# Float32 transposes of rounded values, and unread bf16 products on TensorE, in a two-layer gated attention and FFN kernel

## The chip, the cores and the metric

The kernel runs on one NeuronCore of a Trainium2 chip. The metric is the device time of one launch in microseconds (us): the median of 3 runs of the kernel before is 760.56 us, the lowest 758.46, the highest 766.45.

## The reference, cut to what matters

x is [4, 512, 256] in float32, the context likewise. Two layers are computed, each of a gated cross-attention (16 heads of 16) and a gated feed-forward part. In layer 0 the latter is a mixture of 8 experts with the best two per token, in layer 1 a two-matrix FFN (256 to 1024 to 256) whose weights are rounded to -1, 0, 1 times a scale and whose activations are rounded to whole numbers per token. The rounded activations are what the change touches.

```python
def quant_act(x):
    scale = 127.0 / clip(max(abs(x), axis=-1), 1e-5, None)
    return clip(round(x * scale), -128.0, 127.0) / scale
def bitlinear(x, w): return einsum('bsi,oi->bso', quant_act(x), quant_weight(w))

x = x + tanh(g_xattn[0]) * attention0(layernorm(x), ctx, ctx)
x = x + tanh(g_ffn[0]) * experts(layernorm(x))
x = x + tanh(g_xattn[1]) * attention1(layernorm(x), ctx, ctx)
x = x + tanh(g_ffn[1]) * bitlinear(gelu(bitlinear(layernorm(x), w1)), w2)
```

## The kernel before, in words

There are 8 periods, one for each layer and batch element; periods 0 to 3 are the attention of layer 0, 4 to 7 that of layer 1. A period has 32 half steps, called slots here. `table()` writes the order of all work as one list, and every engine walks this same list and takes what is its own, so that each engine's queue is in the list's order.

In each slot TensorE (PE) does two score products of a later head ("S", line 778, into the three PSUM banks psS, 48 rows each), whose row maxima VectorE (DVE) reduces ("maxima", line 1215, one per product); two transposed score products ("T", line 792, into psT), whose exponentials ScalarE (ACT) writes to pt (line 1024); and in every second slot eight products with the values ("PV", line 806). S runs 12 slots ahead of T, so 12 slots of S alone stand ahead of slot 0 of period 0. There is one psT: the next T waits for the exponential of the one before. S waits for the reduction three products back. After the S of four heads, GpSimd (POOL) splits the maxima into two parts (mp, lines 669 and 672), PE transposes them (line 815, "MT"), ACT copies them to mt (line 1040), and a DMA adds them as rows to the queries, on which T waits.

All other work ("pieces") hangs on fixed slots by `work_table()`. Pieces use the two banks of psX in turn; PE's `bank()` waits until the piece before last has been read out. The pieces that the change and the prediction touch:

- SPLIT (line 731): a projection of keys or queries in float32, which ACT reads out twice (lines 971, 972); POOL subtracts to get the low part (line 595).
- LNC and LNN: the layer norm's numbers on POOL, its application on ACT (line 981, four tiles of 128 tokens, into xn).
- In periods 5 to 7 the FFN of the batch element just attended: XQ at slot 12 (DVE finds each token's scale, lines 1358 to 1368; POOL multiplies and adds a large constant, which rounds, line 678). XI at slot 14: ACT subtracts the constant and writes bf16 (line 1054). XB at slot 15: PE transposes eight 128x128 blocks (line 882), ACT copies them to xit (line 1064). F1 at slot 16: 16 bf16 products of 512 columns (line 903) and four Gelus on ACT (line 1075).
- For each of four token tiles t: HQ at slot 17+3t (DVE lines 1377 to 1387, POOL line 684 rounds hh in place), HS at 19+3t (ACT subtracts the constant and writes bf16 hq, line 1086), HT at 20+3t (eight PE transposes, line 913, and an ACT copy, line 1100), F2 at 21+3t (eight products, line 921; DVE adds, line 1397).

The last stage (NP = 8, after the last head) does the same for the last batch element with nothing beside it. There 45 unread bf16 products (BUSY, line 930) already run on PE.

## Time and profile before

| | us |
|---|---|
| median of 3 runs | 760.56 |
| lowest, highest | 758.46, 766.45 |
| the profiled execution's own time | 767.57 |
| its span (first to last instruction) | 764.9 |
| PE, DVE, ACT, POOL busy in the span | 691.0, 533.3, 445.5, 164.3 |

The profiled execution took 7.01 us more than the median, and 2.67 us of it lie around the span. All rows below are of this one execution. A busy PE is not a PE at its peak, since the records of pipelined products include their latency. The column PEclk is the clock granted to TensorE as a share of 2.4 GHz: 1.00 is 2.4 GHz, 0.50 is 1.2 GHz, and a value between is a mixture in time of the two.

### The profile page before, as it was taken

What the parts mean: (1) busy time and instruction counts of PE and PEld (TensorE: products, weight loads), DVE (VectorE), ACT (ScalarE), POOL (GpSimd) and SP (SyncE); (2) the same over time, 40 slices, a digit from 0 to 9 for tenths busy, and PEclk for the clock granted to TensorE, in tenths of its full rate; (3) what the DMA queues carried; (4) which work ended last, traced back from release to release, by engine and by line L of the source; (5) the groups of instructions that cost most, each with busy time, mean ns of one, the idle gap of its engine ahead of it and who ended that gap; (6) DMA issues with size and microseconds to landing.
All of it is one profiled execution on the core that took longest, in us unless ns stands there. A gap on an engine that the chain in (4) does not pass through costs nothing.

```text
span 764.9 us, 10167 instructions
## 1 busy us (share of the span) xinstructions
PE 691.0 (90%) x3595; PEld 327.5 (43%) x3600; DVE 533.3 (70%) x1140; ACT 445.5 (58%) x570; POOL 164.3 (21%) x300
## 2 busy tenths in 40 slices
PE   4899999899999999998999989998989898987786
PEld 2433333454544545444554545443444344432343
DVE  2767886568886778867887688765786668774334
ACT  2237766763346634664437634567776678658746
POOL 7115333620011210121101410213210311021132
PEclk9769999999999999999999999999999889978999
DMA  7948578430111610323210502126031402200000
GB/s 240 241 128 294 180 250 268 139 80 7 42 43 38 157 29 15 71 84 82 43 43 30 152 16 42 43 79 198 24 80 52 123 3 63 50 2 2 21 8 27
DMA packets 39026, 66.73 MB, mean 87 GB/s; under 512 B 5185, under 2 KB 13889, under 8 KB 38721
## 3 DMA queue, kind: packets, MB, share of 16 engines
q1 hardware_dynamic: 38128, 65.57, 30.2%
q8 instruction: 28, 0.46, 0.3%
q10 hardware_dynamic: 848, 0.53, 0.2%
q14 instruction: 22, 0.17, 0.1%
HBM read 38.29 MB, written 27.26 MB: 86 GB/s over the span
## 4 chain that ended last, share of the span: by engine, by line
PE 59%; DVE 14%; ACT 11%; issue 9%; POOL 8%; POOLq 0%; DVEq 0%; ACTq 0%
PE psO L806 11%; PE psS L778 8%; PE psX L731 7%; PE psT L792 6%; PE psX L867 5%; DVE mx L1215 5%; PE psX L843 4%; PE psX L868 4%; PE psX L869 4%; PE psX L751 3%; ACT pt L1024 3%; POOL parts L595 2%; DVE xs L1346 2%; ACT qf L971 2%; ACT parts L972 1%
## 5 line engine op out<-in xcount | busy, mean ns | idle before, releaser
L1024 ACT ACTIVATE pt<-psT 128x1024 f32<-128x1024 f32 x256 | 261.6, 1022 | 221.2 <-PE psT L792 218.6
L1215 DVE TENSOR_REDUCE mx<-psS 128x1 f32<-128x512 f32 x512 | 325.3, 681 | 84.0 <-PE psS L778 81.6
L778 PE MATMUL psS<-ks,qs 48*128 48x512 f32 x512 | 153.8, 518 | 15.5 <-DVE mx L1215 14.3
L806 PE MATMUL psO<-pt,vg 128*32 128x512 f32 x1024 | 142.0, 627 | 0.1
L792 PE MATMUL psT<-qs,ks 50*128 50x512 f32 x512 | 119.2, 433 | 9.6 <-ACT pt L1024 8.2
L778 PEld LDWEIGHTS psS<-ks,qs 48*128 48x128 f32 x512 | 60.7, 192 | 136.4 <-issue 75.7
L1346 DVE SCALAR_TENSOR_TENSOR xs<-psX,coef,xs 128x256 f32<-128x256 f32 x128 | 61.8, 483 | 32.4 <-PE psX L869 29.2
L595 POOL TENSOR_TENSOR parts<-qf,parts 128x512 fp32r<-128x512 f32 x30 | 38.4, 1280 | 152.5 <-ACT parts L972 152.5
L792 PEld LDWEIGHTS psT<-qs,ks 50*128 50x128 f32 x512 | 52.6, 191 | 28.1 <-ACT pt L1024 25.2
L867 PE MATMUL psX<-moeh,xh 128*128 128x512 f32 x128 | 57.4, 449 | 4.4 <-DVE xs L1346 4.4
L868 PE MATMUL psX<-moel,xh 128*128 128x512 f32 x128 | 51.0, 398 | 0.0
L869 PE MATMUL psX<-moeh,xl 128*128 128x512 f32 x128 | 50.4, 393 | 0.0
L669 POOL CAST mp<-mx 128x16 fp32r<-128x16 f32 x32 | 6.3, 197 | 173.5 <-DVE mx L1215 173.1
L731 PE MATMUL psX<-ctxb,wk 128*128 128x512 f32 x64 | 36.6, 705 | 7.3 <-DMA wk<-in_Wk 7.3
L867 PEld LDWEIGHTS psX<-moeh,xh 128*128 128x128 f32 x128 | 24.2, 189 | 43.6 <-DVE xs L1346 22.6
L981 ACT ACTIVATE xn<-xs,lnw 128x256 f32<-128x256 f32 x60 | 31.8, 591 | 15.2 <-POOL lnw L631 15.1
L806 PEld LDWEIGHTS psO<-pt,vg 128*32 128x32 f32 x1024 | 20.4, 109 | 44.6 <-issue 43.6
L684 POOL TENSOR_SCALAR hh<-hh,am 128x1024 f32<-128x1024 f32 x16 | 17.9, 1119 | 93.7 <-DVE am L1387 93.7
L731 PE MATMUL psX<-xnt,wq 128*128 128x512 f32 x64 | 32.8, 640 | 1.3 <-ACT xnt L994 0.8
L751 PE MATMUL psX<-wv,ctxb 128*128 128x256 f32 x128 | 33.0, 403 | 0.8 <-DVE parts L1171 0.8
L843 PE MATMUL psX<-wo,ont 128*128 128x256 f32 x128 | 31.6, 391 | 0.8 <-ACT ont L1017 0.8
L612 POOL TENSOR_SCALAR lnw<-mv 128x4 f32<-128x4 f32 (+1 forms) x17 | 3.9, 229 | 126.3 <-DVE mv L1138 125.7
(131 smaller groups left out, 764.1 us busy)
## 6 DMA issues: line engine op xcount, KB each, us to landing
ks<-kd SPq DMA_DIRECT2D x64, 192.0 KB, 3.6
qs<-qd SPq DMA_DIRECT2D x64, 192.0 KB, 4.5
kd<-parts SPq DMA_DIRECT2D x16, 512.0 KB, 3.2
qd<-parts SPq DMA_DIRECT2D x16, 512.0 KB, 2.7
kd<-parts SPq DMA_DIRECT2D x16, 256.0 KB, 3.7
qd<-parts SPq DMA_DIRECT2D x16, 256.0 KB, 3.4
ctxb<-in_ctxT SPq DMA_DIRECT2D x7, 512.0 KB, 4.5
xs<-in_x SPq DMA_DIRECT2D x4, 512.0 KB, 6.1
```

The lines of the kernel that those rows point to most:

```text
L731: i = mm(o, w[:, k, c * P:(c + 1) * P], src[:, k, :], start=k == 0, stop=k == NC - 1)
L751: i = mm(o[:, t * D:(t + 1) * D], ctxb[:, p % 2, k, (2 * half + t) * P:(2 * half + t + 1) * P], wv[l][:, k, :], start=k == 0, stop=k == NC ...
L778: mm(psS[:, i % 3, :], qs[at:at + KR, 2 * g + a, k * P:(k + 1) * P], ks[at:at + KR, 2 * g + a, :], start=True, stop=True).then_inc(pe_s, 1)
L792: i = mm(psT[:, r, :], ks[at:at + KR + MP, 2 * g + half, k * P:(k + 1) * P], qs[at:at + KR + MP, 2 * g + half, :], start=True, stop=True)
L806: i = mm(psO[32 * j:32 * j + 32, :], vg[:, p % 2, k, g * GH + j, :], pt[:, s % RING, j, :], start=k == 0, stop=k == NT - 1, tile_position= ...
L843: i = mm(o[:, t * D:(t + 1) * D], ont[:, k, tt * P:(tt + 1) * P], wo[l][:, k, :], start=k == 0, stop=k == NC - 1)
L867: mm(o, xh[:, k, tok], moeh[:, k, at], start=k == 0, stop=False)
L868: mm(o, xh[:, k, tok], moel[:, k, at], start=False, stop=False)
L869: i = mm(o, xl[:, k, tok], moeh[:, k, at], start=False, stop=k == NC - 1)
L1024: a(pt[:, G % RING, 2 * half:2 * half + 2, :], psT[:], ACT.Exp, scale=SCALE).then_inc(a_exp, 1)
L1215: v.tensor_reduce(mx[:, w // GH % 2, r, col:col + 1], psS[:, i % 3, :], AX.X, ALU.max).then_inc(v_max, 1)
L1346: v.scalar_tensor_tensor(out=xs[:, b, t, :], in0=o[:, k * D:(k + 1) * D], scalar=coef[:, t, e:e + 1], in1=xs[:, b, t, :], op0=ALU.mult, op ...
```

## The change

XI and HS go. PE transposes the rounded float32 values as they are (xn and hh, with the large constant in them), in twice the bytes, so that XB and HT become two pieces of four blocks each; ACT subtracts the constant while it reads PSUM and writes bf16. XB stands at slots 14 and 15 instead of 15, HT at 19+3t and 20+3t instead of 20+3t. The buffers hq and xi are gone, and xh has its own place in SBUF. Two new kinds exist on PE alone. WARM multiplies 512 columns of vg's bytes, as bf16, into psO: 20 ahead of the first S, then 3 after each of the 12 slots of S alone (36). FILL multiplies columns of w1q into the next bank of psX, after waiting until that bank has been read out, at 11 slots of each of periods 5, 6 and 7 (20 products a period, 60 in all). Nothing reads what they write.

```diff
@@ work_table(), periods of layer 1
             put(p, 12, ("XQ", (0, NT)))
-            put(p, 14, ("XI", (0, NT)))
-            put(p, 15, ("XB", (0, NT)))
+            put(p, 14, ("XB", (0, 1, 0, NT)))
+            put(p, 15, ("XB", (1, 2, 0, NT)))
...
                 put(p, 17 + 3 * t, ("HQ", (t,)))
-                put(p, 19 + 3 * t, ("HS", (t,)))
-                put(p, 20 + 3 * t, ("HT", (t,)))
+                put(p, 19 + 3 * t, ("HT", (t, 0)))
+                put(p, 20 + 3 * t, ("HT", (t, 1)))
...
+        if l:
+            for s, k in ((9, 2), (10, 2), (11, 3), (12, 2), (14, 2), (17, 1), (18, 3), (20, 2), (22, 1), (24, 1), (28, 1)):
+                put(p, s, ("FILL", (k,)))
+    for s in range(2 * LEAD):
+        put(lead, 2 * H - 2 * LEAD + s, ("WARM", (3,)))
...
-    put(NP, 6, ("HS", (0,)))
     for t in range(NT):
-        if t + 1 < NT:
-            put(NP, 6, ("HS", (t + 1,)))
-        put(NP, 6, ("HT", (t,)))
+        put(NP, 6, ("HT", (t, 0)), ("HT", (t, 1)))
@@ table(), ahead of the first slot
+    out += [("WARM", (20,))]
@@ PE
-            def xb(t0, t1):
-                o = bank("XB").bitcast(BF16)
+            def xb(c0, c1, t0, t1):
+                o = bank("XB")
                 w = (t1 - t0) * P
-                if due(a_xi, n("XB") + 1):
-                    pe.wait_ge(a_xi, n("XB") + 1)
-                for c in range(NC):
+                if due(p_xq, n("XQ tiles")):
+                    pe.wait_ge(p_xq, n("XQ tiles"))
+                for c in range(c0, c1):
...
-                        i = nc.tensor.transpose(o[:, at:at + P], xi[:, t, c * P:(c + 1) * P], identb[:])
+                        i = nc.tensor.transpose(o[:, at:at + P], xn[:, t, c * P:(c + 1) * P], identf[:])
...
+            def ht(t, half):
+                o = bank("HT")
+                if due(p_hq, n("HT") // 2 + 1):
+                    pe.wait_ge(p_hq, n("HT") // 2 + 1)
+                for k in range(NT):
+                    at = (half * NT + k) * P
+                    m = nc.tensor.transpose(o[:, k * P:(k + 1) * P], hh[:, t, at:at + P], identf[:])
...
+            def warm_up(k):
+                if due(c_pool, POOL_ALL):
+                    pe.wait_ge(c_pool, POOL_ALL)
+                for i in range(k):
+                    mm(psO[:], identb[:], vg[:, 1].rearrange("p t h d -> p (t h d)").bitcast(BF16)[:, 0:S],
+                       start=True, stop=True)
+
+            def fill(k):
+                b = n.piece() % 2
+                if due(*last[b]):
+                    pe.wait_ge(*last[b])
+                for i in range(k):
+                    mm(psX[:, b, :], identb[:], w1q[:, 0, 0:S], start=True, stop=True)
@@ ACT
-                a(xit[:, :, t0 * P:t1 * P], o.rearrange("p (c t) -> p c t", c=NC), ACT.Copy).then_inc(a_xb, 1)
+                a(xit[:, c0:c1, t0 * P:t1 * P], o.rearrange("p (c t) -> p c t", c=c1 - c0), ACT.Identity, bias=negm[:]
+                  ).then_inc(a_xb, 1)
...
-                a(hqt[:, i % 2].rearrange("p k t -> p (k t)"), o, ACT.Copy).then_inc(a_ht, 1)
+                a(hqt[:, i // 2 % 2, half * NT:(half + 1) * NT, :].rearrange("p k t -> p (k t)"), o, ACT.Identity,
+                  bias=negm[:]).then_inc(a_ht, 1)
```

How PE's queue changes at the head. Before, the transposes of the second layer norm were followed at once by the S of four heads (psS) and the transpose of their maxima (psX from mp):

```order
L762 MATMUL psX<-identf,xn 128x128 x8
L778 MATMUL psS<-ks,qs 128x512 x18
L815 MATMUL psX<-identf,mp 32x128
L778 MATMUL psS<-ks,qs 128x512 x8
L792 MATMUL psT<-qs,ks 128x512 x2
```

Now the same place reads (the pair of S and three products then repeats, up to the T of slot 0):

```order
L762 MATMUL psX<-identf,xn 128x128 x8
L926 MATMUL psO<-vg,identb 128x512 x20
L778 MATMUL psS<-ks,qs 128x512 x2
L926 MATMUL psO<-vg,identb 128x512 x3
L778 MATMUL psS<-ks,qs 128x512 x2
```

Twenty unread products stand between the transposes and the first S, and three behind every pair of S.

PE's queue in periods 5 and 6 from slot 14 to slot 16 before (the eight bf16 transposes at the end of slot 15):

```order
L778 MATMUL psS<-ks,qs 128x512 x2
L792 MATMUL psT<-qs,ks 128x512 x2
L778 MATMUL psS<-ks,qs 128x512 x2
L792 MATMUL psT<-qs,ks 128x512 x2
L806 MATMUL psO<-pt,vg 32x512 x4
L882 MATMUL psX<-identb,xi 128x128 x8
L778 MATMUL psS<-ks,qs 128x512 x2
```

and now:

```order
L778 MATMUL psS<-ks,qs 128x512 x2
L792 MATMUL psT<-qs,ks 128x512 x2
L880 MATMUL psX<-identf,xn 128x128 x4
L934 MATMUL psX<-w1q,identb 128x512 x2
L778 MATMUL psS<-ks,qs 128x512 x2
L792 MATMUL psT<-qs,ks 128x512 x2
L806 MATMUL psO<-pt,vg 32x512 x4
L880 MATMUL psX<-identf,xn 128x128 x4
L778 MATMUL psS<-ks,qs 128x512 x2
```

The first four transposes moved one slot earlier, ahead of S, T and PV of slot 15, and two unread products stand behind them.

ACT's queue for the first token tile, from the exponentials of slots 18 and 19 to that of slot 21, before:

```order
L1024 ACTIVATE pt<-psT 128x1024 x2
L1086 ACTIVATE hq<-hh,negm 128x1024
L1024 ACTIVATE pt<-psT 128x1024
L1040 ACTIVATE mt<-psX 32x128
L1100 ACTIVATE hqt<-psX 128x1024
L1024 ACTIVATE pt<-psT 128x1024 x2
```

and now (L1038 is the exponential, L1054 the copy to mt):

```order
L1038 ACTIVATE pt<-psT 128x1024 x2
L1099 ACTIVATE hqt<-psX,negm 128x512
L1038 ACTIVATE pt<-psT 128x1024
L1054 ACTIVATE mt<-psX 32x128
L1099 ACTIVATE hqt<-psX,negm 128x512
L1038 ACTIVATE pt<-psT 128x1024 x2
```

Two operations of 1024 columns became two of 512, at the same places.

## Rows read from the trace of the kernel before

**Rows 1.** The page: the chain that ended last, share of the span by engine.
```profile
PE 59%; DVE 14%; ACT 11%; issue 9%; POOL 8%; POOLq 0%; DVEq 0%; ACTq 0%
```

**Rows 2.** Stretches: length, busy PE, PEld, DVE, ACT, POOL (instructions), PEclk, DMA share, GB/s.
```profile
28.50:44.00 15.50, 14.32 (x29) 6.55 (x28) 14.03 (x24) 0.99 (x3) 0.42 (x2) 0.50 0.95 238
44.00:57.00 13.00, 12.15 (x34) 4.26 (x35) 7.81 (x18) 6.40 (x8) 2.23 (x2) 0.68 0.31 105
...
517.30:529.80 12.50, 9.93 (x51) 3.39 (x47) 7.11 (x14) 8.84 (x13) 5.25 (x12) 0.86 0.73 222
...
538.30:570.60 32.30, 29.06 (x201) 12.92 (x200) 28.63 (x59) 24.87 (x28) 7.63 (x9) 0.95 0.17 41
...
590.40:609.00 18.60, 16.45 (x78) 5.85 (x77) 13.83 (x30) 11.82 (x16) 5.94 (x15) 0.82 0.34 92
617.60:651.30 33.70, 30.48 (x201) 13.15 (x200) 28.74 (x59) 24.90 (x28) 5.31 (x8) 0.90 0.15 39
676.80:697.40 20.60, 15.53 (x59) 5.30 (x57) 8.08 (x16) 14.83 (x18) 2.26 (x6) 0.67 0.01 2
```

**Rows 3.** Chain of waits at the head: start us, us, what.
```profile
27.47 1.06 PE psX L762 x8
...
29.33 9.66 DVE mx L1215 x16
...
45.18 3.72 PE psX L731 x4
```

**Rows 4.** PE's timeline, three projections: start, us, line, operation.
```profile
51.59 3.07 PE L731 MATMUL psX<-ctxb,wk 128*128 128x512 f32 x4
...
58.01 1.88 PE L731 MATMUL psX<-xnt,wq 128*128 128x512 f32 x4
...
599.68 2.98 PE L731 MATMUL psX<-ctxb,wk 128*128 128x512 f32 x4
```

**Rows 5.** PE's timeline: transposes and unread products.
```profile
67.00 0.63 PE L762 MATMUL psX<-identf,xn 128*128 128x128 f32 x4 [0.77 <-ACT xn L981]
...
736.73 6.21 PE L930 MATMUL psO<-w1q,identb 128*128 128x512 bf16 x28
...
753.62 0.62 PE L913 MATMUL psX<-identb,hq 128*128 128x128 bf16 x8 [0.30 <-ACT hq L1086]
```

**Rows 6.** Groups by form, ACT: busy us, mean ns, idle before.
```profile
L1086 ACT ACTIVATE hq<-hh,negm 128x1024 bf16<-128x1024 f32 x16 | 18.1, 1139 | 0.0
L1100 ACT ACTIVATE hqt<-psX 128x1024 bf16<-128x1024 bf16 x16 | 16.3, 1019 | 1.6 <-PE psX L913 1.5
L971 ACT ACTIVATE qf<-psX,bkc 128x512 f32<-128x512 f32 x16 | 11.0, 688 | 19.2 <-PE psX L731 19.1
...
L1054 ACT ACTIVATE xi<-xn,negm 128x512 bf16<-128x512 f32 x2 | 1.4, 722 | 0.7 <-POOL xn L678 0.7
```

**Rows 7.** Timeline of period 6, from the key projection's low part to slot 16.
```profile
604.04 1.27 POOL L595 TENSOR_TENSOR parts<-qf,parts 128x512 fp32r<-128x512 f32 x1 [5.79 <-ACT parts L972]
...
605.30 1.84 POOL L678 TENSOR_SCALAR xn<-xn,am 128x256 f32<-128x256 f32 x4
...
609.01 0.50 PE L778 MATMUL psS<-ks,qs 48*128 48x512 f32 x2
```

**Rows 8.** Waits of PE, 506 to 729 us: total, times, longest.
```profile
PE psX L921 <- ACT hqt L1100: 3.6, 6, 0.8
```

**Rows 9.** Timeline of period 5 around slots 20 and 21.
```profile
547.20 0.25 ACT L1040 ACTIVATE mt<-psX 32x128 fp32r<-32x128 f32 x1
...
547.34 0.50 PE L778 MATMUL psS<-ks,qs 48*128 48x512 f32 x2
```

**Rows 10.** Timeline of period 7, slot 13, and the S of slots 17 and 18.
```profile
679.87 0.50 PE L792 MATMUL psT<-qs,ks 50*128 50x512 f32 x2 [1.60 <-ACT pt L1024]
...
697.41 0.50 PE L778 MATMUL psS<-ks,qs 48*128 48x512 f32 x2 [1.20 <-ACT hh L1075]
...
699.07 0.50 PE L778 MATMUL psS<-ks,qs 48*128 48x512 f32 x2
```

More of the change, by code:

```diff
@@ L905, in f1 @@
                 m.then_inc(pe_f1, 1)
-            def ht(t):
-                i = n("HT")
-                o = bank("HT").bitcast(BF16)
-                if due(a_hq, i + 1):
-                    pe.wait_ge(a_hq, i + 1)
-                for k in range(HID // P):
-                    m = nc.tensor.transpose(o[:, k * P:(k + 1) * P], hq[:, i % 2, k * P:(k + 1) * P], identb[:])
+            def ht(t, half):
[5 more added lines that the diff above has]
+                    m = nc.tensor.transpose(o[:, k * P:(k + 1) * P], hh[:, t, at:at + P], identf[:])
                 m.then_inc(pe_ht, 1)
@@ L933, in _ @@
                   "MT": m_transpose, "NT": o_transpose, "OT": ot, "OP": op, "RT": router, "ME": experts, "XB": xb,
-                  "F1": f1, "HT": ht, "F2": f2, "BUSY": keep_busy}, n)
+                  "F1": f1, "HT": ht, "F2": f2, "BUSY": keep_busy, "WARM": warm_up, "FILL": fill}, n)
         @block.scalar
@@ L979, in ln @@
                     act.wait_ge(pe_xt, n("XT"))
+                if due(pe_xb, n("XB")):
+                    act.wait_ge(pe_xb, n("XB"))
                 for t in range(t0, t1):
@@ L1045, in router, with xb @@
                 a(rt[:, 2], rt[:, 1], ACT.Exp).then_inc(a_rexp, 1)
[L1047 removed]
+            def xb(c0, c1, t0, t1):
+                o = bank()
                 if due(c_pool, POOL_ALL):
                     act.wait_ge(c_pool, POOL_ALL)
[L1050 to L1058 removed]
                 if due(pe_xb, n("XB") + 1):
@@ L1076, in f1 @@
                   scale=am[:, 2, t:t + 1]).then_inc(a_f1, 1)
-            def hsub(t):
-                i = n("HS")
-                if due(p_hq, i + 1):
-                    act.wait_ge(p_hq, i + 1)
-                if due(pe_me, n("ME")):
-                    act.wait_ge(pe_me, n("ME"))
-                if due(pe_ht, i - 1):
-                    act.wait_ge(pe_ht, i - 1)
-                a(hq[:, i % 2, :], hh[:, t, :], ACT.Identity, bias=negm[:]).then_inc(a_hq, 1)
             def gelu_table():
@@ L1091, in gelu_table, with ht @@
                 a(junk[:], negm[:], ACT.Gelu).then_inc(a_junk, 1)
-            def ht(t):
-                o = bank().bitcast(BF16)
+            def ht(t, half):
+                o = bank()
                 i = n("HT")
```

43 lines of the change are left out of this document (15 added, 28 removed).

## Prediction

> **What bounds the kernel now.** I read the page's chain of waits first: 59% of the span is PE's work and 9% issue, so the order of PE's queue sets the time [rows 1]. Next come the stretches with the granted clock, since half of the change is unread products. The stretches that the change can reach and that are not at the upper level (2.4 GHz, 1.00) are these. The head runs at 1.2 GHz from 28.5 to 44 us and mostly so until 57 us; in the last three periods 0.86, 0.95, 0.82, 0.90 and 0.67 are granted over stretches of 12.5, 32.3, 18.6, 33.7 and 20.6 us [rows 2]. A stretch of length l at clock c spent 2 x (1 - c) x l at the lower level: 3.5 + 3.2 + 6.7 + 6.7 + 13.6 = 33.7 us in the last three periods, and 15.5 + 8.3 = 23.8 us in the head. At most half of such time can come back, and only where PE's columns are what the slot waits for. The reader is to see in [rows 2] also that DVE is busy 28.6 of 32.3 us and 28.7 of 33.7 us in the second halves of periods 5 and 6, so there the clock is not alone. Before the low stretch of period 7 PE had sat 1.60 us behind the layer norm on ACT [rows 10].
>
> **Prices.** An unread product costs 6.21 / 28 = 0.22 us at the upper level [rows 5]; at the lower one, half the clock, 0.44 is my estimate from it. Four float32 transposes take 0.63 us alone [rows 5], eight take 1.06 us [rows 3], so each further one costs 0.11; eight bf16 ones take 0.62 us, at most 0.08 each. Forty transposes a period thus cost 1 to 2 us more PE time in all, depending on how much of the 0.62 is latency. ACT's read-out with a bias of 512 float32 columns from PSUM is bounded by L971: 0.69 us [rows 6]. A bf16 output is not shown for it. Half of L1100's 1.02 is the lower end, 0.51; L971 and the 0.12 by which L1086 exceeds L1100 give the upper, 0.81. I take 0.69, the nearest in form. Per token tile ACT then works 2 x 0.69 = 1.38 instead of 1.14 + 1.02 = 2.16 us, 0.78 less.
>
> **Head.** The chain there is: transposes until 28.5, first S at once, then 16 maxima on DVE in 9.66 us, 0.60 each [rows 3]. DVE is busy 14.03 of 15.5 us [rows 2], so S at half clock cost nothing. The block of 20 lies on this chain with no cover: 4.4 us if the clock is up throughout, 8.8 if it is down throughout. It starts after a thin stretch, and the clock should rise on the way: I take 5.5. Three products behind a pair of S need 0.66 us beside two maxima of 1.2 us; at full clock a pair of S leaves room for them, except behind the transpose of the maxima, where DVE has run dry: +0.6. What comes back are the first projections of slots 0 and 2: 3.72 and 3.07 us against 1.88 at full clock [rows 3, 4], that is 1.8 + 1.2, and about 0.5 on S, T and PV between them: -3.5. Head: +2.6 us, between +1.5 (4.4 and 0.6 less 3.5) and +5.9 (8.8 for the block).
>
> **Slots 9 to 16.** The products at 9 to 12 add 9 x 0.22 = 2.0 us. In period 5 slots 9 and 10 are PE's own, but slot 12 then waits for POOL's maxima; in 6 and 7 PE waits for DVE there. I cost them at nothing; without that cover it is 2 us a period. With the clock up, the key projection takes 1.9 instead of 2.98 us in period 6 [rows 4], and its stretch starts about 1.1 us earlier. But PE's next piece is now XB's first half at slot 14, and it waits for POOL's rounding, which is queued behind the projection's low part on POOL. Before, slot 16 began 609.01 - 607.14 = 1.87 us after the rounding ended (605.30 + 1.84) [rows 7]. Now four transposes (0.45), two products (0.44), S, T and PV of slot 15 (1.66, the distance of the S of slots 17 and 18 in [rows 10]), and four more transposes (0.45) follow it, 3.0 us. S and T of slot 15 and everything behind wait in PE's queue. Of 1.7 us gained ahead of POOL, 1.1 are given back: -0.6 in period 6, -0.5 in period 5. If the clock was up anyway, this is +1.1. Period 7 has no projection and no V, so ACT's chain of table load and four Gelus bounds slot 16; its 20.6 us at 0.67 should give 1.7 (0.5 if the clock still falls once or twice after the wait of 1.60, 3.5 if it holds): -1.7.
>
> **Slots 17 to 31.** The low stretch of period 6 made it 33.7 against 32.3 us in period 5 [rows 2]. With four products at 17 and 18 both should lose their low time: -0.4 in period 5, and -0.4 more the difference of 1.4, -1.8, in period 6. PE's waits for hqt were 3.6 us in six cases [rows 8]; the shorter read-out and HS's going take about 1.2 of them from each of periods 5 and 6. Against this, FILL at slots 20 and 28 waits for ACT's copy to mt, which ends at 547.45, 0.11 us after the next S had started, and its 0.44 then stand in front of S and T, which others wait for: +0.5 and +0.4 [rows 9]. Left: -0.3 each. In period 7, where S has run out, T waits for the exponential and PE's slots with PV get 0.45 of transposes more: +0.6.
>
> **Last stage.** XI's 0.72 us [rows 6] leaves the serial chain twice, a read-out longer by 0.1 comes in; HS leaves too, but two banks of psX now carry two halves per tile, and each half waits for the read-out two before: -0.3 us, between -2 and +1.
>
> **Sum.** Head +2.6; period 5: -0.5 - 0.4 - 0.3 = -1.2; period 6: -0.6 - 1.8 - 0.3 = -2.7; period 7: -1.7 + 0.6 = -1.1; end -0.3. Together -2.7 us, so the profiled execution's 767.57 us would be 764.9. The median of the runs, 760.56, lies 7.01 us below that execution, and probably had less low clock; I apply the sum to it and rounded downward: 757.5 us.
>
> The Trainium skill, page TensorE: Matmul & The Clock Gate, section Part 4: PE-mode transpose, says that transposes don't count as work for the clock. No row here isolates transposes, so nothing tests it. By that rule the doubled transpose time in slots 14, 15 and 19 on would thin out exactly the places that the unread products are to fill, and the clock would go on falling; that is the third rival below.
>
> **Rivals.** About 1%, 7.6 us, is what a measurement of this kernel can tell from no change.
> - The clock was the bound, and comes back whole. For it: 33.7 us at the lower level, PE 90% busy. Half of it is 16.9, the waits for hqt add 3.6 at most; with two thirds of that, -13.7, and the head's +2.6, the time is 749.5 us. Against it: DVE's 89% and POOL's queue.
> - Slower: the 60 products and 120 transposes find no cover. 13.2 us and some 5 us (120 times 0.04) of PE time stand in PE's queue, the head takes 2.6, the clock gives 9 back and the waits for hqt 2.8: +9, 769.5 us. It decides at slots 9 to 12, 18 and 20: if T starts later there than the exponential before it ends, each product costs 0.22. For it: 59% of the chain is PE. Against it: PE's waits lie just where most products are put.
> - The change doesn't do what it says: the clock falls in periods 5 to 7 as before, since the new wait for POOL at slot 14 and that of 1.60 us [rows 10] remain. Then only head and added work are left: 764.5 us.
> - In the head the clock does not rise under the block: then the block takes 8.8, each of 12 pairs needs 3 x 0.44 for its products and some 0.9 for its S (512 columns at 1.2 GHz, twice), 2.2 us against 1.2, and nothing comes back: +20.8 in the head in place of +2.6, 776 us. Unlikely, since long float32 products at 45 us brought it back.
>
> **How the numbers follow.** Forecast 0.46, whole clock 0.28, no cover 0.12, clock as before 0.11, head at half clock 0.03. Faster by over 1% is the second and a little of the first: 0.30; slower by over 1% the third and the last: 0.15; within 1%: 0.55. The forecast's own range is 753 to 763; over the others 748.5 to 766.
>
> **What would show it.** In the profile after: the block of 20 at the head 4.4 to 6.5 us long, T of slot 0 5 to 6 us later, the projections of slots 0 and 2 at 1.9 us. A clock of 1.00 in the stretches of periods 5 and 6, a wait of PE of 1 to 2 us for xn at slot 14, slot 16 beginning 3 us after POOL's rounding. PE waiting for mt at slot 20. ACT's read-out at 0.69 us. Wrong it would be if slots 9 to 12 grow by their products, if period 7 stays at 0.67, or if the second halves of periods 5 and 6 fall under 31 us.

## The result and the profile after

| | before | after |
|---|---|---|
| median, us | 764.56 (20 runs) | 768.55 (20 runs) |
| lowest, highest | 758.46, 769.55 | 764.59, 773.66 |
| profiled execution, its span | 767.57, 764.9 | 773.66, 771.9 |

The ratio is 1.0061, 95% interval 1.0039 to 1.0084: slower by 0.6%, which lies within the 1% called "no change" in the prediction, but outside its range of 748.5 to 766 and on the other side of its 757.5. The median of before over 20 runs is 4.0 us above that of the 3 runs on which the forecast stood. The ratios and clocks of this document leave out executions that took over 1.5% more than the fastest of their kernel (e1 had one of 804.23 us).

What the reader must hold together is that the clock did rise. Over the timed executions the mean granted clock of the kernel before is 0.964, of the changed one 0.989: 2 x 0.025 x 765 is some 38 us fewer at 1.2 GHz. The time rose all the same, so the clock that came back was worth less than what the change costs.

The stretches of periods 5 to 7 show where. The borders are the starts of the exponentials of slots 0 and 16, the last one that of slot 31 of period 7; columns as in [rows 2]. The kernel before:

```profile
487.68:530.81 43.13, 39.79 (x201) 16.99 (x202) 28.89 (x57) 29.91 (x43) 12.42 (x28) 0.96 0.39 120
530.81:571.40 40.59, 36.96 (x234) 17.49 (x234) 30.54 (x63) 31.98 (x36) 7.63 (x9) 0.96 0.20 45
571.40:610.04 38.64, 35.29 (x179) 14.87 (x179) 26.69 (x52) 25.04 (x33) 7.58 (x18) 0.91 0.34 92
610.04:652.10 42.06, 38.45 (x234) 17.78 (x234) 30.65 (x63) 32.09 (x35) 5.31 (x8) 0.92 0.18 43
652.10:689.29 37.19, 33.10 (x170) 13.78 (x169) 26.43 (x52) 22.82 (x29) 5.11 (x16) 0.88 0.10 22
689.29:726.68 37.39, 28.42 (x184) 11.99 (x189) 14.64 (x36) 30.61 (x33) 4.89 (x6) 0.94 0.04 12
```

The changed kernel, same view and borders:

```profile
497.52:541.70 44.18, 41.03 (x210) 18.06 (x212) 28.73 (x57) 29.44 (x42) 12.49 (x28) 0.96 0.37 117
541.70:583.34 41.64, 38.90 (x241) 18.86 (x244) 30.98 (x63) 29.79 (x35) 7.65 (x9) 1.00 0.18 44
583.34:621.21 37.87, 34.57 (x188) 14.64 (x190) 26.65 (x52) 24.57 (x32) 7.61 (x18) 1.00 0.32 89
621.21:662.90 41.69, 38.94 (x241) 18.86 (x244) 30.98 (x63) 29.80 (x35) 5.33 (x8) 1.00 0.22 49
662.90:697.79 34.89, 31.92 (x179) 13.61 (x180) 26.34 (x52) 22.26 (x29) 5.14 (x16) 1.00 0.10 22
697.79:733.93 36.14, 30.25 (x191) 13.72 (x198) 14.83 (x36) 27.97 (x33) 4.92 (x6) 1.00 0.04 13
```

Five of six stretches now have the full clock, and the second half of period 5 is longer than before by 1.05 us at 1.00 against 0.96. Together 236.4 against 239.0 us, a gain of 2.6, although the time at the lower level in them went from 34 to 3.4 us. Even this gain is that of one profile against one. e12, a run below whose periods 5 to 7 are those of the kernel before, took 235.5 us for the same six stretches:

```profile
sum 235.47, PE 208.63 PEld 92.16 DVE 157.38 ACT 172.19 POOL 43.12; mean PE 34.77 PEld 15.36 DVE 26.23 ACT 28.70 POOL 7.19
```

So the old code of these periods takes 235.5 or 239.0 us, depending on where the clock falls in it, and the changed code at 236.4 us is no gain that one pair of profiles can show.

The head lost more. The chain of waits of the changed kernel there:

```profile
30.10 1.06 PE psX L762 x8
31.16 0.42 PE psO L926
...
31.81 5.36 PE psO L926 x18
37.17 0.48 PE psS L778
37.64 9.88 DVE mx L1215 x16
...
48.23 0.27 PE psX L815
...
53.32 0.23 PE psT L792 x2
53.54 1.93 PE psX L731 x4
```

Beside [rows 3]: the block of 20 stands as a piece of its own on the chain, 31.16 to 37.17, 6.0 us (the clock is 0.73 over it). The 16 maxima that follow take 9.88 us (9.66 before); the first projection is down from 3.72 to 1.93. The exponential of slot 0 starts at 53.58 instead of 45.21, 8.4 us later, and slot 0 lasts 3.07 instead of 4.87 us. Of the 8.4, 2.6 lie ahead of the block, where the transposes start at 30.10 instead of 27.47 (the last section comes back to them). Period 1, on which nothing of the change falls, was 2.6 us longer in this execution: its slots 5 to 7, at low clock, took 4.2 us more, its slot 15 1.6 us less.

The spans of the two profiles differ by 7.0 us. From slot to slot this is: 2.6 ahead of the head, 4.5 for the head (5.7 until slot 0, 1.8 back in it, 0.6 lost in slot 2), 2.6 in period 1, -2.6 in periods 5 to 7, -0.3 behind them, and 0.2 of small differences and rounding. The first and the third, 5.2 us, fall on code that the change doesn't touch.

In period 5, slot 14, the timeline of the changed kernel shows the wait that took XI's place:

```profile
532.94 1.28 POOL L595 TENSOR_TENSOR parts<-qf,parts 128x512 fp32r<-128x512 f32 x1 [3.44 <-ACT parts L984]
...
534.21 1.86 POOL L678 TENSOR_SCALAR xn<-xn,am 128x256 f32<-128x256 f32 x4
...
536.12 1.07 PE L880 MATMUL psX<-identf,xn 128*128 128x128 f32 x4 [1.79 <-POOL xn L678]
...
537.98 0.79 PE L778 MATMUL psS<-ks,qs 48*128 48x512 f32 x2
538.57 0.63 PE L792 MATMUL psT<-qs,ks 50*128 50x512 f32 x2
...
539.24 1.02 ACT L1038 ACTIVATE pt<-psT 128x1024 f32<-128x1024 f32 x1 [1.26 <-PE psT L792]
```

PE waits 1.79 us for POOL. Right behind this wait the clock falls, from 536.2 to 539.6 us: the transposes, S and T run at half clock (S 0.79 and T 0.63 us; 0.50 and 0.40 where the clock is up), and ACT stands still for 1.26 us. Slot 14 lasts 4.87 instead of 2.82 us. The waits of PE and the prices of the new operations, periods 5 to 7 (total, times, longest; then busy us, mean ns):

```profile
PE psX L880 <- POOL xn L678: 3.8, 3, 1.8
...
PE psX L934 <- ACT mt L1054: 1.7, 4, 0.5
PE psX L919 <- ACT hqt L1099: 1.7, 6, 0.4
```
```profile
L1099 ACT ACTIVATE hqt<-psX,negm 128x512 bf16<-128x512 f32 x24 | 16.4, 684 | 5.0 <-PE psX L911 5.0
```

The read-outs take 0.684 us (forecast 0.69), and the waits for hqt are down from 3.6 [rows 8] to 1.7 us, but 3.8 for POOL and 1.7 for mt are new.

### The profile page after: what moved, and what is told of

Same layout as the page of the kernel before. It is cut to its first block, busy times and chain, and to the rows that moved or that the text cites. A ratio compares the mean times of both kernels' runs of the same rounds, so it can differ in the third digit from the quotient of the medians.

```text
span 771.9 us, 10364 instructions
## 1 busy us (share of the span) xinstructions
PE 705.5 (91%) x3697; PEld 336.2 (44%) x3716; DVE 535.4 (69%) x1140; ACT 433.3 (56%) x568; POOL 164.5 (21%) x300
## 4 chain that ended last, share of the span: by engine, by line
PE 61%; DVE 13%; ACT 10%; issue 8%; POOL 8%; POOLq 0%; DVEq 0%; ACTq 0%
PE psO L806 11%; PE psS L778 8%; PE psX L731 6%; PE psT L792 6%; PE psX L867 5%; DVE mx L1215 5%; PE psX L843 4%; PE psX L868 4%; PE psX L869 4%; PE psX L751 3%; ACT pt L1038 3%; POOL parts L595 2%; DVE xs L1346 2%; ACT qf L983 2%; PE psX L919 2%
## 5 line engine op out<-in xcount | busy, mean ns | idle before, releaser
L1038 ACT ACTIVATE pt<-psT 128x1024 f32<-128x1024 f32 x256 | 262.0, 1024 | 227.8 <-PE psT L792 225.6
L778 PE MATMUL psS<-ks,qs 48*128 48x512 f32 x512 | 143.2, 498 | 12.0 <-DVE mx L1215 9.3
L806 PE MATMUL psO<-pt,vg 128*32 128x512 f32 x1024 | 139.1, 616 | 0.1
L792 PE MATMUL psT<-qs,ks 50*128 50x512 f32 x512 | 116.7, 423 | 5.7 <-ACT pt L1038 4.8
L778 PEld LDWEIGHTS psS<-ks,qs 48*128 48x128 f32 x512 | 55.4, 184 | 121.3 <-issue 74.1
L792 PEld LDWEIGHTS psT<-qs,ks 50*128 50x128 f32 x512 | 51.7, 187 | 19.7 <-ACT pt L1038 16.1
L731 PE MATMUL psX<-ctxb,wk 128*128 128x512 f32 x64 | 34.1, 661 | 7.2 <-DMA wk<-in_Wk 7.2
L843 PE MATMUL psX<-wo,ont 128*128 128x256 f32 x128 | 33.4, 407 | 0.8 <-ACT ont L1031 0.8
```

Source lines behind the costliest of these rows:

```text
L731: i = mm(o, w[:, k, c * P:(c + 1) * P], src[:, k, :], start=k == 0, stop=k == NC - 1)
L778: mm(psS[:, i % 3, :], qs[at:at + KR, 2 * g + a, k * P:(k + 1) * P], ks[at:at + KR, 2 * g + a, :], start=True, stop=True).then_inc(pe_s, 1)
L792: i = mm(psT[:, r, :], ks[at:at + KR + MP, 2 * g + half, k * P:(k + 1) * P], qs[at:at + KR + MP, 2 * g + half, :], start=True, stop=True)
L806: i = mm(psO[32 * j:32 * j + 32, :], vg[:, p % 2, k, g * GH + j, :], pt[:, s % RING, j, :], start=k == 0, stop=k == NT - 1, tile_position= ...
L843: i = mm(o[:, t * D:(t + 1) * D], ont[:, k, tt * P:(tt + 1) * P], wo[l][:, k, :], start=k == 0, stop=k == NC - 1)
L1038: a(pt[:, G % RING, 2 * half:2 * half + 2, :], psT[:], ACT.Exp, scale=SCALE).then_inc(a_exp, 1)
```

## The experiments

"Clock" is the mean granted clock of a kernel's timed executions. Ratios are to the kernel before, run on the same chip; the runs were spread over several chips, so ratios are compared here and not medians.

| run | head | periods 5 to 7 | median | ratio (95%) | clock |
|---|---|---|---|---|---|
| after | 20 + 3 | f32, all FILL | 768.55 | 1.0061 (1.0039-1.0084) | 0.989 |
| e15 | 20 + 3 | f32, all FILL, again | 770.25 | 1.0059 (1.0025-1.0093) | 0.988 |
| e4 | - | f32, no FILL | 763.97 | 0.9992 (0.9964-1.0020) | 0.969 |
| e1 | - | f32, all FILL | 766.55 | 1.0004 (0.9980-1.0028) | 0.977 |
| e3 | 20 + 3 | f32, no FILL | 765.47 | 1.0016 (0.9990-1.0043) | 0.985 |
| e2 | 3 | f32, all FILL | 763.40 | 0.9983 (0.9962-1.0004) | 0.989 |
| e7 | 20 | f32, all FILL | 769.02 | 1.0074 (1.0045-1.0103) | 0.979 |
| e12 | 20 + 3 | old, no FILL | 765.66 | 1.0015 (0.9989-1.0040) | 0.979 |
| e5 | - | f32, early FILL | 760.33 | 0.9951 (0.9926-0.9976) | 0.976 |
| e6 | 3 | f32, early FILL | 759.43 | 0.9959 (0.9927-0.9992) | 0.986 |
| e8 | - | f32, XB at 15, no FILL | 762.95 | 0.9993 (0.9966-1.0021) | 0.967 |
| e9 | - | f32, XB at 15 in 5, 6, early FILL | 755.18 | 0.9891 (0.9853-0.9928) | 0.980 |
| e10 | 3 | as e9 | 756.70 | 0.9883 (0.9841-0.9925) | 0.992 |
| e13 | - | old, all FILL | 759.33 | 0.9922 (0.9889-0.9955) | 0.980 |
| e11 | - | old, early FILL | 757.25 | 0.9907 (0.9881-0.9933) | 0.978 |
| e14 | - | old, FILL 9 to 12 | 756.86 | 0.9875 (0.9841-0.9908) | 0.978 |
| e16 | 3 | old, early FILL | 755.68 | 0.9867 (0.9833-0.9901) | 0.990 |

"f32" are the float32 transposes, "old" the bf16 ones with XI and HS; "early FILL" is slots 9 to 12, 17 and 18, and "all FILL" the eleven slots of the change. "20" and "3" are the products at the head, the block and those behind each pair of S.

**The head.** Four runs take parts of the change away.

```diff
e1, e4:    -    out += [("WARM", (20,))]
e1, e4:    -    for s in range(2 * LEAD): put(lead, 2 * H - 2 * LEAD + s, ("WARM", (3,)))
e3, e4:    -            for s, k in ((9, 2), ... (28, 1)): put(p, s, ("FILL", (k,)))
e2:        -    out += [("WARM", (20,))]
```

> The changed kernel without both kinds of unread products at the head (neither the 20 nor the 3 behind each pair of S); float32 transposes and FILL stay. Theory A (the 20 products lie uncovered on the head's chain, some 6 us, and give back under 2.5 us; the last three periods gain 2.6 us): the head is as in the kernel before, T of slot 0 near 44.5 us, slots of S still 1.2 us per pair, and the time is 2 to 4 us below the kernel before, ratio 0.995 to 0.998. Rival R1 (the clock's phase in layer 0, where period 1 was 2.6 us longer though nothing was changed in it, is what made the change slower): the time of the last three periods and of period 1 stays long, ratio 1.000 to 1.006. Rival R2 (the rest of the change costs, by products or half pieces in the last three periods): ratio over 1.003.

> The changed kernel without the block of 20 unread products, with the 3 behind each pair of S. Theory A: the 3 alone find S at the lower clock (first S right behind the transposes, at about 28.5 us), a pair of S and three products then take over 1.2 us until the clock rises, so the head is 1 to 4 us shorter than in the changed kernel; ratio to the kernel before 0.996 to 1.003. Rival (the 3 never bring the clock up by themselves): each pair takes 2.2 us, head some 10 us longer than in the kernel before, ratio 1.010 or more. Rival (the 3 bring it up as the 20 do, and the 20 are pure loss): first maxima 6 us earlier than in the changed kernel and the projection of slot 0 at 1.9 us, ratio 0.993 to 0.997.

> The changed kernel without FILL (60 unread products in periods 5 to 7); float32 transposes and both WARM stay. Theory A (FILL keeps the clock up at slots 9 to 18 and costs about 1 us a period behind them): the clock falls again in periods 5 to 7 (granted 0.82 to 0.95 in the stretches of rows 2), the three periods come out 2 to 5 us longer than in the changed kernel, ratio to the kernel before 1.007 to 1.013. Rival R3 (FILL is what costs in the last three periods, and the transposes gain by themselves): 1 to 4 us shorter than the changed kernel, ratio 1.000 to 1.005.

> The changed kernel with the float32 transposition alone, no unread product added anywhere. Theory A (transposing in float32 takes POOL's wait to slot 14 and the half pieces fall on slots 27 to 29; two ACT passes go): between -2 and +3 us in the last three periods, head as before, ratio 0.998 to 1.004. Rival R2 (the transposes and half pieces cost): ratio 1.004 or more. Rival R3 (they gain and FILL costs): ratio under 0.997.

The chain of e3, where the clock was up throughout the block:

```profile
28.63 4.32 PE psO L923 x20
32.95 0.48 PE psS L775 x2
33.43 9.88 DVE mx L1212 x16
```

4.32 us is the block's price at full clock. The exponential of slot 0 starts at 49.35 in e3 and at 44.92 in e4, 4.4 us apart; slot 0 gives back 1.80 (3.07 against 4.87), and nothing else of the head differs: +2.6 us net. With the 3 alone (e2) the clock comes up at the third pair; slot 0's exponential starts at 46.41, 1.5 us later than in e4, and the same 1.80 come back: -0.3 net. So the 20 buy nothing that the 3 don't. e2 came out as theory A had it in its ratio and at its first pairs of S, which take 1.6 and 2.1 us until the clock rises; in what the 20 add, its last rival was right: without them too the projection of slot 0 takes 1.93 us. For e1 theory A doesn't hold: the time is no lower than that of before, so the rest of the change gains nothing either. Its ratio, 1.0004, is in the range of R1 and below that of R2. R1's reason is not borne out, since slots 0 to 15 of period 1 took 42.51 us in e1's profile, no more than the 42.75 of the kernel before; R2's, that the rest costs, is what e13 below shows. e3 was expected above the changed kernel and came out below it: rival R3, FILL costs. Theory A was right in that the clock falls without FILL (0.96, 0.92 and 0.95 in the first halves of periods 5 to 7), but not in what this is worth. e4's ratio came out as theory A had it, no gain and no loss that can be measured; its periods 5 to 7 take 235.1 us, beside 239.0 in the profile of before and 235.5 in e12's.

Two more runs close the head.

```diff
e7 (after):    -    for s in range(2 * LEAD): put(lead, 2 * H - 2 * LEAD + s, ("WARM", (3,)))
e12 (before):  +    out += [("WARM", (20,))]
               +    for s in range(2 * LEAD): put(lead, 2 * H - 2 * LEAD + s, ("WARM", (3,)))
```

> The changed kernel without the 3 unread products behind each pair of S, with the block of 20. Theory A2 (the block's 4.4 to 6 us lie bare, whatever follows): the first S comes 4.4 to 6 us after the end of the transposes, S alone does not hold the clock up, slot 0 is as long as in the kernel before (4.9 us), so nothing comes back: ratio to the kernel before 1.004 to 1.010. Rival (the block alone keeps the clock up until slot 0): slot 0 at 3.1 us, ratio 1.002 to 1.006 with a head as in the changed kernel.

> The kernel before with both kinds of unread products at the head (20, and 3 behind each pair of S) and nothing else. Theory A2 (the block lies bare at 4.4 to 6 us, 1.8 to 2.9 us come back in slots 0 and 2): T of slot 0 4.4 to 6.5 us later, 1.5 to 4.5 us slower, ratio 1.002 to 1.006. Rival (the head gives back what it costs): ratio 0.998 to 1.001. Rival (it costs more than the block): ratio over 1.007.

The stretch 37 to 54 us of e7:

```profile
37.00:54.00 17.00, 16.13 (x30) 7.09 (x30) 13.44 (x25) 2.37 (x4) 0.42 (x2) 0.50 0.32 69
```

Behind the block PE is busy 16.1 of 17 us with S and later T, and yet at 0.50: S alone does not hold the clock, and slot 0 is again 4.87 us. The block alone is pure loss, ratio 1.0074. e12 is below the range that theory A2 gave (1.0015, its profile has slot 0's exponential at 49.40); with its interval, between -1 and +3 us is what it shows. The whole head thus costs +0.15% on the kernel before (e12), +0.24% between e4 and e3 and +0.57% between e1 and the changed kernel; each of these is uncertain by 0.3 to 0.4%, and their ranges overlap at 0.24 to 0.40%.

**Which products of FILL cost.** From e1 to e3 (with and without FILL, float32 transposes) the slots of periods 5 and 6 at full clock differ at slot 20 by 0.90, at 24 by 0.18, at 28 by 0.49 us and at no other from 17 to 31 by more than 0.07 us once 17 and 18 (+0.33, -0.33) are taken together. The reason stands in the timeline of the changed kernel, slot 20:

```profile
557.77 0.25 ACT L1054 ACTIVATE mt<-psX 32x128 fp32r<-32x128 f32 x1
...
558.07 0.60 PE L934 MATMUL psX<-w1q,identb 128*128 128x512 bf16 x2 [0.46 <-ACT mt L1054]
558.61 0.50 PE L778 MATMUL psS<-ks,qs 48*128 48x512 f32 x2
558.95 0.40 PE L792 MATMUL psT<-qs,ks 50*128 50x512 f32 x2
...
559.39 1.03 ACT L1038 ACTIVATE pt<-psT 128x1024 f32<-128x1024 f32 x1 [0.80 <-PE psT L792]
```

and in that of e3, same place:

```profile
548.81 0.50 PE L775 MATMUL psS<-ks,qs 48*128 48x512 f32 x2
549.04 0.25 ACT L1051 ACTIVATE mt<-psX 32x128 fp32r<-32x128 f32 x1
...
549.19 0.50 PE L789 MATMUL psT<-qs,ks 50*128 50x512 f32 x2
```

Without the two products S starts 0.23 us before the copy to mt, with them it starts 0.84 us behind it: the wait costs as much as the products, and ACT's exponential stands behind both. The same wait stands at slot 12 of period 6 (0.43 us for mt), which takes 2.52 us with its two products and 2.20 in e4 and e12 without them. e5, with nothing at the head, drops those of slots 14, 20, 22, 24 and 28; e6 is e5 with the 3 at the head.

```diff
-            for s, k in ((9, 2), (10, 2), (11, 3), (12, 2), (14, 2), (17, 1), (18, 3), (20, 2), (22, 1), (24, 1), (28, 1)):
+            for s, k in ((9, 2), (10, 2), (11, 3), (12, 2), (17, 1), (18, 3)):
```

> As the kernel without unread products at the head (e1_no_warm), and FILL only at slots 9, 10, 11, 12, 17 and 18 (13 products a period); those of slots 14, 20, 22, 24 and 28 go. Theory A2 (formed on the first four runs: of FILL's products those of slots 9 to 12, 17 and 18 lie behind DVE or ACT and cost nothing, those of slots 14, 20, 24 and 28 stand in front of S and T and cost 0.4, 0.9, 0.2 and 0.5 us, and the clock stays up in slots 17 to 31 without them): second halves of periods 5 and 6 at 40.2 us and of period 7 at 35.3 us, as without FILL, first halves of 6 and 7 near 37.5 and 34.5 us; 4 to 5 us below e1_no_warm, ratio to the kernel before 0.992 to 0.996. Rival (the products behind slot 18 are needed for the clock): the second halves fall to the lower level again for 3 us or more and take over 41 us, ratio 0.998 or more.

> As e5_fill_early, with the 3 unread products behind each pair of S at the head (without the block of 20). Theory A2: the head as in e2_no_block (T of slot 0 some 1.5 us later, slot 0 by 1.8 us shorter), so within 1 us of e5_fill_early; ratio to the kernel before 0.991 to 0.996. Rival (the products at the head also keep later falls of the clock away, as the mean clocks 0.987 of e2_no_block and 0.973 of e1_no_warm suggest): 2 us or more below e5_fill_early. Rival (they cost as in the changed kernel): 2 us or more above it.

As A2 had it: second halves of periods 5, 6 and 7 at 40.16, 40.15 and 35.23 us with the clock at 1.00, ratio 0.9951. e6 gives the same, so the 3 are neutral within the noise.

**The place of the transposition of xn.** e8 moves it in periods 5 to 7, e9 and e10 in periods 5 and 6 alone.

```diff
-            put(p, 14, ("XB", (0, 1, 0, NT)))
-            put(p, 15, ("XB", (1, 2, 0, NT)))
+            put(p, 15, ("XB", (0, 1, 0, NT)), ("XB", (1, 2, 0, NT)))
```

> As e4_transposes_alone, both halves of the float32 transposition of xn at slot 15 (PE's wait for POOL's rounding back where it was, behind S and T of slot 14). Theory A2 (the place of the first half at slot 14 makes S and T of slots 14 and 15 wait for POOL and lets the clock fall there): slots 14 and 15 of periods 5 and 6 get back 0.8 us in period 5 and up to 3.6 us in period 6, ratio 1 to 4 us under e4_transposes_alone, 0.994 to 0.998. Rival (the wait for POOL only moves to slot 15 or 16): slots 14 to 16 take the same sum, ratio as e4_transposes_alone, 0.998 to 1.001.

> As e5_fill_early (no unread products at the head, FILL at slots 9, 10, 11, 12, 17, 18), and in periods 5 and 6 both halves of the transposition of xn at slot 15, in period 7 at 14 and 15. Theory A2 (the first half at slot 14 makes S and T of slots 14 and 15 wait for POOL: e8_xb_at_15 had 1.0 us less in period 5, and in period 6 3.8 us with the clock up in it, in period 7 0.5 us more): 1.5 to 2.5 us below e5_fill_early, ratio to the kernel before 0.990 to 0.994. Rival (the wait moved behind slot 14 lets the clock fall in slots 17 to 31, as it did once in e8_xb_at_15, 41.5 instead of 40.1 us in period 5): ratio as e5_fill_early or over, 0.995 to 0.998.

> As e9_early_and_xb_mix, with the 3 unread products behind each pair of S at the head. Theory A2 (the 3 cost 1.5 us ahead of slot 0 and give 1.8 back in it): within 1.5 us of e9_early_and_xb_mix, ratio to the kernel before 0.989 to 0.994. Rival (products at the head that keep the clock up also change later falls): more than 2 us away from it in either direction.

e8's profile had the gain (slots 14 and 15 of period 5 4.41 instead of 5.40 us, of period 6 4.35 instead of 8.18, where the clock no longer fell), and lost 1.3 of it in the second half of period 5, where the clock fell once; over 12 executions its ratio shows nothing and lies in the range of the rival, not of A2. On top of early FILL the same move shows: 0.9891 and 0.9883, beyond the end of the expected range. The first half of period 5 is 41.20 us at full clock in e9, 43.66 with one fall at slot 14 in e5. All seven profiles with XB's first half at slot 14 and products at slots 9 to 12 (after, e15, e1, e2, e5, e6, e7) have this fall in period 5; of the six that have the products and no transposition at slot 14 (e9, e10, e11, e13, e14, e16) none has it.

**The old transposes with FILL.**

```diff
e11 (before):  +            for s, k in ((9, 2), (10, 2), (11, 3), (12, 2), (17, 1), (18, 3)): put(p, s, ("FILL", (k,)))
e13 (before):  + all eleven slots       e14 (before):  + (9, 2), (10, 2), (11, 3), (12, 2) only
e16: e11 and   +    for s in range(2 * LEAD): put(lead, 2 * H - 2 * LEAD + s, ("WARM", (3,)))
```

> The kernel before with its bf16 transposes and XI and HS, and FILL at slots 9, 10, 11, 12, 17, 18 alone. Theory A2 (both parts are needed: FILL holds the clock up to slot 14, the float32 transposes without XI and HS take the waits of slots 19 to 26 away): the first halves gain as in e5_fill_early (the clock at 1.00 in slots 10 to 15), slots 19 to 26 keep their waits for hqt and hq and may fall to the lower level: 1 to 3 us better than the kernel before, ratio 0.996 to 0.999, above e5_fill_early. Rival (all of e5's gain is FILL's): ratio 0.993 to 0.996. Rival (FILL without the float32 transposes loses): ratio over 1.000.

> The kernel before with its bf16 transposes, and FILL at all eleven slots as in the changed kernel (20 products a period), nothing at the head. Theory A3 (the products of slots 9 to 12, 17 and 18 bring 0.9907; those of slots 14, 20, 24 and 28 stand in front of S and T and cost 1.2 to 2.0 us a period; the float32 half piece at slot 14 costs the rest): 3.5 to 6 us above e11_old_transposes_fill_early, ratio to the kernel before 0.995 to 0.999. Rival (with the old transposes the late products fall into PE's waits for hqt and cost nothing): ratio 0.989 to 0.993. Rival (they cost as on the float32 transposes and the transposes themselves cost nothing): ratio 0.9995 to 1.002, as e1_no_warm.

> The kernel before with its bf16 transposes, and FILL at slots 9, 10, 11 and 12 only (9 products a period). Theory A3 (these hold the clock until slot 16, those of 17 and 18 hold it in slots 19 to 21): first halves of periods 5 to 7 as in e11_old_transposes_fill_early (41.5, 36.6, 34.3 us), second halves of 5 and 6 fall again for 3 us or so and take 40.6 instead of 39.7 us; ratio 0.991 to 0.996. Rival (9 to 12 are enough for both): ratio 0.989 to 0.992, second halves at 39.7 us at 1.00.

> As e11_old_transposes_fill_early, with the 3 unread products behind each pair of S at the head. Theory A3 (they cost 1.5 us ahead of slot 0 and give 1.8 back in it, as in e2_no_block and e6_threes_and_fill_early): within 1.5 us of e11_old_transposes_fill_early, ratio 0.988 to 0.993. Rival (in a kernel whose clock is up everywhere else they pay): ratio under 0.988. Rival (they cost): ratio over 0.993.

> The changed kernel once more, unaltered, for a second profile. Theory A3 (the 2.6 us at the very start and those of period 1 in the first profile are the clock's phase in untouched code, not the change): the exponential of slot 0 starts near 49.4 us if the clock is up under the block, 51 us if it is half down, instead of 53.58 us; slots 16 to 31 of periods 5 to 7 take 41.65, 41.65 and 36.1 us as in the first profile; ratio 1.003 to 1.009. Rival (they belong to the change): exponential of slot 0 again after 53 us.

In these runs the function that writes the products is taken over with them. Here A2 missed: e11 was expected above e5 and is below it, 0.9907, below both ranges given. The six stretches of e11:

```profile
486.21:527.68 41.47, 39.64 (x210) 17.27 (x211) 28.95 (x57) 29.88 (x42) 12.46 (x28) 1.00 0.36 121
527.68:567.42 39.74, 36.68 (x239) 17.42 (x238) 30.36 (x63) 31.76 (x36) 7.64 (x9) 1.00 0.20 52
567.42:604.05 36.63, 34.56 (x188) 14.55 (x188) 26.85 (x52) 25.03 (x32) 7.59 (x18) 1.00 0.29 79
604.05:643.73 39.68, 36.64 (x239) 17.41 (x238) 30.35 (x63) 31.73 (x36) 5.31 (x8) 1.00 0.24 62
643.73:678.05 34.32, 31.69 (x179) 13.31 (x178) 26.49 (x52) 22.72 (x29) 5.10 (x16) 1.00 0.11 23
678.05:714.08 36.03, 27.76 (x189) 11.88 (x193) 14.59 (x36) 30.50 (x34) 4.89 (x6) 1.00 0.04 12
```

All six at 1.00, 227.9 us in all against 239.0 before and 235.5 in e12. And three of e4, the float32 transposes alone (first and second half of period 5, second of period 7):

```profile
489.05:532.97 43.92, 39.61 (x201) 17.09 (x202) 28.71 (x57) 29.36 (x43) 12.47 (x28) 0.96 0.37 118
532.97:573.11 40.14, 37.76 (x235) 18.58 (x235) 30.76 (x63) 29.65 (x36) 7.65 (x9) 1.00 0.20 48
...
688.90:724.16 35.26, 29.21 (x185) 13.02 (x189) 14.84 (x36) 27.87 (x33) 4.91 (x6) 1.00 0.04 13
```

At full clock the second half of period 5 takes 39.74 us with the old transposes and 40.14 with the new ones, of period 7 36.03 against 35.26: the new ones cost 0.4 where S and T fill PE, and gain 0.8 where S has run out. Period 6 reads like 5. The larger part of the difference to e5 is in the first halves of periods 5 and 6 (43.66 and 37.39 us there, 41.47 and 36.63 here), where XI's pass on ACT at slot 14 left PE free to go on with slot 15, and XB's first half does not. With both halves at slot 15 (e9) they take 41.20 and 36.78 us: what is left is the place of the transposition, not its type.

e13 settles the square. Its second halves take 40.76, 40.78 and 36.93 us, 1.0, 1.1 and 0.9 above e11's: that is what the late products cost on the old transposes, 3.0 us. Its ratio, 0.9922, is in the range of the rival that has them free, since A3 expected 3.5 to 6 us and counted slot 14 in. There the two products are free with the old transposes: slots 14 to 16 of period 5 take 12.99 us in e11 and e13 alike. The four corners without anything at the head:

| | no FILL | all FILL |
|---|---|---|
| old transposes | 1 | 0.9922 |
| float32 transposes | 0.9992 | 1.0004 |

e14: products at 9 to 12 alone do as well (0.9875, below both ranges given; the second half of period 6 fell once, 40.56 us, that of period 5 not). e16, 0.9867, is in the range of the rival in which the 3 pay, but its interval reaches 0.9901, and e6 against e5 and e10 against e9 show no such gain; it is not to be told from e14, e10 and e9; in its profile the clock fell once more in period 7 (37.16 us for the first half instead of 34.32), so early FILL makes falls rarer and does not end them. These four are the fastest, by 1.1 to 1.3% against the kernel before; e11, e13, e5 and e6 beat both kernels too, by 0.4 to 0.9%. e15 is taken up in the last section.

## Why the prediction was wrong

In short: periods 5 to 7 were forecast at -5.0 us and gave between -2.6 (against the profile of before) and +0.9 (against e12's), and the largest miss in them lies in slots 17 to 31 of periods 5 and 6, forecast at -0.3 us a period beside the clock and measured at +1.8 and +1.9 us against e11, whose clock is up as well. Of the signs that the prediction named for itself, the block's length, the wait for xn, the waits for mt, the read-outs at 0.69 us and the clock in five of six stretches came out, and none of those against it; the start of slot 0 (8.4 us later, not 5 to 6) and the projection of slot 2 (3.6 us) did not. So the waits were seen; it is their prices that were wrong.

Step by step, with the terms as the prediction put them.

1. *The level.* The sum was applied to 760.56, the median of three; the median of 20 is 764.56. 4.0 of the 11.0 us by which the forecast was low are this. "Probably had less low clock" fits, since the profiled execution took longer than 18 of the 20 timed ones; but a median of three that spreads over 8 us was taken as exact.
2. *Head, +2.6.* Block 5.5: measured 4.3 with the clock up (e3), 6.0 with it half down (after). Behind MT +0.6: from the start of the transpose of the maxima to that of T it was 5.06 us before (39.69 to 44.75) and is 5.09 (48.23 to 53.32), so nothing. Given back 3.5: measured 1.8. The projection of slot 2 was counted as certain; it ran at full clock in e4 with nothing at the head (slot 2 3.07 us) and at half clock in the changed kernel. The net in e3 against e4 is +2.6, the number forecast, by luck: the errors of -1.2, -0.6 and +1.7 cancel. In the changed kernel's profile it is +4.5, since the block met a low clock and slot 2 gave nothing back. That the 3 hide beside two maxima was right.
3. *Slots 9 to 12 at nothing:* right but for 0.3 us at slot 12 of period 6, as e11 and e13 show. The gain ahead of slot 14 was right too: slots 0 to 13 of periods 5 and 6 are 1.6 us shorter each than in the profile of before, forecast 1.6 and 1.7.
4. *Slots 14 to 16, the wait for POOL.* Priced at 1.1 us, and measured at 0.9 in e4's period 5 (slots 14, 15 and 16 +0.34, +0.43, +0.12), where the clock stayed up. This step failed in that the wait was priced by its queue alone: the clock also falls behind it. Then slots 14 and 15 cost 2.7 us more than before in period 5 of the changed kernel and 3.6 in period 6 of e4. The prediction weighed this for period 7, and for periods 5 and 6 in its rival "clock as before" alone. In the changed kernel's profile it makes 1.7 us of miss in period 5 and none in period 6, where the clock stayed up.
5. *Slots 17 to 31, "-0.3 each": the largest failed step.* The changed kernel misses the forecast by 1.6 us in each of periods 5 and 6 here. "+0.5 and +0.4" for the products at slots 20 and 28: the mechanism, the wait for mt in front of S and T, was right and its size was 1.4, plus 0.2 at slot 24. "About 1.2 of the waits for hqt" back: they fell by 1.9 us over the three periods, but the slots did not get shorter by it: with the clock up in both, slots 19, 21, 27 and 29 are longer by 0.3 to 0.8 us in e4 than in e11 and the others shorter by less in sum, so that the second halves are 0.4 us longer. That a wait of PE shrinks was taken as time gained; which wait takes its place in each slot is not traced here, except in slot 27, where S waits 0.9 us for the maxima. The clock alone was priced too low, at 0.4 and 1.8 us: the second halves are 0.85 and 2.4 us shorter in e11 than before. Period 7: +0.6 forecast, about +0.1 measured (28.13 against 28.01 us from slot 17 on).
6. *Period 7, slots 12 to 16, -1.7:* 3.7 in fact, the upper end that was named (3.5); *last stage -0.3:* -0.28.
7. Of the rivals, "clock as before" (764.5) did not come true: the clock rose. "No cover" (769.5) came nearest in number and in sign, with its place half right: the early products are covered, the late ones and the block are not. The rule of the Trainium skill beside it (page TensorE: Matmul & The Clock Gate, section Part 4: PE-mode transpose: transposes don't count as work for the clock) would have the doubled transposes thin out slots 19 on. e4, with these transposes and no unread product, has 1.00 in the three second halves where the kernel before had 0.96, 0.92 and 0.94 and e12, with the same bf16 transposes, 0.96, 0.96 and 1.00; one profile each, and e8 fell once in period 5. So the runs give that consequence no support here, and none of them tests the rule itself.

What moves the time, in one line of ratios, each measured on top of the one before: all FILL on the old transposes -0.78%, the float32 transposes on that +0.82%, both kinds at the head on that +0.57%, together +0.61%. In another order the parts are others: the float32 transposes cost 0.82% on all FILL, 0.44% on early FILL (e5 against e11) and nothing without FILL (e4), where the clock falls in the first halves of all three periods with either kind.

## What to carry to other kernels

Unread products are worth placing only in slots where a trace shows TensorE waiting for another engine anyway; three placements here were free or nearly so (behind DVE-bound pairs of S, slots 9 to 12, 17 and 18), and three on the chain (a block ahead of the first S, behind a wait for a copy with S and T queued after it, behind a wait for POOL) took back everything. Where a slot is bound by VectorE or by a wait, a higher clock gives nothing back: from the first S to the T of slot 0 it was 16.2 us before, at 1.2 GHz, and 16.1 in e3, at 2.4. Judge such a change by the length of stretches at equal clock, and with more than one profile of the kernel before, not by the granted clock: the changed kernel and e16 have the same mean clock, 0.989 and 0.990, and lie 1.9% apart in time. When a pass on another engine is removed, ask what TensorE does in its place: the pass at slot 14 was cheap because TensorE had S, T and the products with the values of slot 15 to do before it waited 0.5 us for it.
